# The output loop of an attention and expert kernel: stores moved from ScalarE to SyncE's queue, one load a unit earlier, and the spread of reciprocals ahead of a load

## The chip, the cores and the metric

The kernel runs on 1 core of a Trainium2 chip. The metric is the device time of one execution in microseconds (us), the median of several.

## What is computed

`x` is 8 sequences of 1024 tokens with 256 features. The reference normalises each token and adds to `x` an attention part (16 heads of 64) and a part of 64 experts, 8 to a token, with one shared expert:

```python
x = L0_attn_y
xn = _layernorm(x, axis=-1)
# _L0_attn_ref: per head h, out_h = softmax(q_h k_h^T / 8) v_h; result = concat(out_h) @ Wo.T + bo
# _L0_ffn_ref: routed experts (silu(g) * u @ w_down, weighted, summed over a token's experts) + shared expert
x = x + _L0_attn_ref(xn, ...) + _L0_ffn_ref(xn, ...)
```

## The kernel before, in words

A first stage normalises, routes and computes the values and the shared expert. Then come 64 (`NP`) pairs of heads, 8 to a sequence, in 65 steps written once in `step` for each engine: step s computes the scores, exponentials and value products of pair s, finishes pair s-1 (`fin`) and prepares the following ones. Step 63 is `LAST`, step 64 is `NP`, which has only the finish of pair 63. One expert is computed beside each pair; GpSimd adds its rows to the tensor `moe` in HBM by an indirect DMA. Normalised outputs of a pair go to `ot` in HBM (`store`, L1682, from `out_raw`). To normalise, the sums' reciprocals (`recip`, VectorE, L1385) are spread over the partitions by eight small DMAs (`spread_out`, L1675, into `sum_all`), and VectorE multiplies (L1402).

The output loop multiplies `ot` with Wo. It runs over 16 units (`UNITS`) of 512 tokens; unit u is half `u % 2` of sequence `u // 2`, and its buffers have the parity `par = u % 2`. For each unit:

- SyncE loads the unit's outputs (`load_output`, L1803: two DMAs of 1 MB into `ot32`), and the input x and the expert part of a unit (`load_rest`, L1809 and L1810: 0.5 MB each). In step 63 it loads units 0 and 1, in step 64 units 2 and 3 and the rest of units 0 and 1; in `output()` it loads in each turn unit u and the rest of unit u-2.
- ScalarE rounds the outputs to their high half (`split_high`, L1288, into what were `q_full` and `k_full`; in step 63, for unit 0, `split_piece`, L1280), VectorE subtracts to have the low half (`split_low`, L1483, into `q_rest` and `k_rest`).
- TensorE (`tokens`, L1168) makes for each of 4 groups of 128 tokens 24 matmuls of 128x256, in the order high (`q_full`), low (`q_rest`), high (`k_full`), low (`k_rest`): 96 a unit. Behind unit 0 it makes a constant row (L1180, L1181), which ScalarE copies (L1305).
- GpSimd adds x and expert part (L1641, `rest`), VectorE adds the constant (L1491) and the two banks of PSUM (L1499, into `y`).
- ScalarE issues one DMA of 0.5 MB that stores the unit (`store`, L1296). Each buffer (`ot32`, `x_out`, `moe_sb`, `rest`, `y`) is there twice.

The order is set by each engine's own queue and by semaphores. ScalarE's turn for unit u waits for TensorE's unit u-2 (`y_filled`), splits unit u, and then waits for VectorE's last add of unit u-1 (`y_ready`) to store it; the split of unit u+1 is queued behind that. VectorE's turn is `split_low(u)` twice, then `add_rest(u-1)`. SyncE's `load_output` of unit u waits for the load before it and for `ot_low`, the low halves of unit u-2; `load_rest` of unit u-2 is queued behind it and waits for GpSimd's add of two units before. In step 63 SyncE issues, in this order, the shift DMAs (L1662), `load_output(0, 0, 0)`, a wait for its landing, `load_output(0, 1, 1)` and `spread_out(62)`. VectorE's work in that step behind the reciprocals is: a copy out of PSUM, the first norm (L1402), the gate of the expert (L1408, L1412), the second norm, three sums of exponentials (L1477), the low half of Wo (L1456), another copy (L1394), a low half of unit 0 (L1483), four more sums, and the other low half. TensorE's sums over partitions (L1018) and its last product with the values (L1003) follow these, then unit 0.

Of the kernel before, what the change touches and what calls it, by code (L numbers as in the profile page):

```python
# [26 lines left out]
B, N, D = 8, 1024, 256  # L27
# [4 lines left out]
NP = B * PAIRS  # L32
# [10 lines left out]
UNIT = 4  # L43
UNITS = TILES // UNIT

HIGH, LOW = 0, 1
DMA = 16
# [5 lines left out]
def alone(engine, met, *waits):  # L53
    waits = [(sem, v if isinstance(v, int) else engine.to_reg(v)) for sem, v in waits]
    engine.wait_ge(*met)
    for sem, value in waits:
        engine.wait_ge(sem, value)


def known(v, least):  # L60

    return isinstance(v, int) and v < least
# [651 lines left out]
def is_step(s, n):  # L714

    return isinstance(s, int) and s == n
# [4 lines left out]
LAST = NP - 1  # L721
# [59 lines left out]
def attention_stage(nc, ctx, io, keep):  # L781
# [76 lines left out]
    out_v = io["out"].rearrange("(u t p) d -> u p t d", p=P, t=UNIT)  # L858
# [347 lines left out]
    def _(act):  # L1206
# [81 lines left out]
                nc.scalar.copy(ot(par, HIGH, batch), ot32[par][:, batch * BATCH:(batch + 1) * BATCH]  # L1288
                               ).then_inc(ot_high, 1)

        def store(v, par):

            if not known(v, 1):
                act.wait_ge(y_stored, DMA * v)
            act.wait_ge(y_ready, 2 * (v + 1))
            act.dma_start(out_v[bass.ds(v, 1)].rearrange(parts), y[:, par]).then_inc(y_stored, DMA)  # L1296

        def output():
            def unit(u, par):
                act.wait_ge(y_filled, 2 * (u - 1))  # L1300
                split_high(u, par)
                store(u - 1, 1 - par)

            act.wait_ge(const_filled, 1)
            nc.scalar.copy(const[:], const_ps).then_inc(const_ready, 1)  # L1305
            store(0, 0)
            unit(2, 0)
            unit(3, 1)
            with act.Fori(2, UNITS // 2) as i:
                unit(i * 2, 0)  # L1310
                unit(i * 2 + 1, 1)
            store(UNITS - 1, 1)
            act.wait_ge(y_stored, DMA * UNITS)

        def empty(p):

# [27 lines left out]
    def _(dve):  # L1344
# [141 lines left out]
        def add_rest(u, par):  # L1486

            dve.wait_ge(rest_ready, u + 1)
            if known(u, 1):
                dve.wait_ge(const_ready, 1)  # L1490
            nc.vector.tensor_tensor(rest[:, par], rest[:, par],  # L1491
                                    const[:].rearrange("p (o d) -> p o d", o=1).to_broadcast([P, UNIT, D]), ALU.add
                                    ).then_inc(rest_full, 1)
            if not known(u, 2):
                dve.wait_ge(y_stored, DMA * (u - 1))
            dve.wait_ge(rest_full, u + 1)
            for n in range(2):
                dve.wait_ge(y_filled, 2 * u + n + 1)
                nc.vector.tensor_tensor(y[:, par, 2 * n:2 * n + 2, :],  # L1499
                                        psum[:, banks[par][n], :].rearrange("p (t d) -> p t d", d=D),  # L1500
                                        rest[:, par, 2 * n:2 * n + 2, :], ALU.add).then_inc(y_ready, 1)
# [152 lines left out]
    def _(sp):  # L1654
# [50 lines left out]
        def load_values(p, pp):  # L1705
            sp.dma_start(v_sb[:, pp], one(io["v"], p, "p t c", "(o p) t c")).then_inc(v_loaded, DMA)
# [14 lines left out]
        def step(s, par, flags):  # L1721
            fin, att, nxt, prj = flags
            loads = prj and not (isinstance(s, int) and s == NP - 3)
            p, pp = s + 1, 1 - par
            if is_step(s, LAST - 1):
                sp.wait_ge(lows_ready, 4 * NP)
                sp.dma_start(wo32[:], io["wo"].rearrange("(h p) d -> p h d", p=P)).then_inc(loaded_w, DMA)
                sp.dma_start(bv[:], io["bv"]).then_inc(loaded_b, DMA)
                sp.dma_start(bo[:], io["bo"]).then_inc(loaded_b, DMA)
            if nxt:  # L1730
                waits = [(lows_ready, 4 * (s + 2))]
                if not known(s, 0):
                    waits.append((placed, DMA * SHUFFLES * (s + 1)))
                if not known(s, 1):
                    waits.append((probs_ready, SCORES * s))
                alone(sp, (standing, 1), *waits)
                place(pp)
            if att:
                shift_out(s, par, 1)
            if is_step(s, LAST):  # L1740
                for half in range(2):
                    sp.wait_ge(out_stored[half], DMA * PAIRS)
                sp.wait_ge(placed, DMA * SHUFFLES * NP)
                sp.wait_ge(quad_filled, QUADS * NP)
                load_output(0, 0, 0)
                for n in range(2):
                    sp.wait_ge(ot_loaded[n], DMA)
                load_output(0, 1, 1)
            if nxt:
                waits = []  # L1750
                if not known(s, 0):
                    waits.append((experts_loaded, 3 * DMA * (s + 1)))
                if not known(s, 1):
                    waits.append((y_weighted, s))
                alone(sp, (standing, 1), *waits)
                load_expert(p, pp)
            if nxt:
                waits = []
                if not known(s, 0):
                    waits.append((v_loaded, DMA * (s + 1)))  # L1760
                if not known(s, 1):
                    waits.append((pv_done, 4 * s))
                alone(sp, (standing, 1), *waits)
                load_values(p, pp)
            if fin:
                spread_out(s - 1)
            if is_step(s, NP):
                sp.wait_ge(pv_done, 4 * NP)
                sp.wait_ge(sums_added, 14 * NP - 7)
                sp.wait_ge(last_sums, 7)  # L1770
                sp.wait_ge(scattered, DMA * NP)
                load_rest(0, 0)
                for n in range(2):
                    sp.wait_ge(ot_loaded[n], 2 * DMA)
                sp.wait_ge(ot_low, 2)
                load_output(1, 0, 0)
                sp.wait_ge(xm_loaded, 2 * DMA)
                load_rest(1, 1)
                for n in range(2):
                    sp.wait_ge(ot_loaded[n], 3 * DMA)  # L1780
                sp.wait_ge(ot_low, 4)
                load_output(1, 1, 1)
            if loads:

                alone(sp, (standing, 1), (w_loaded, 2 * DMA * (s + 3)), (lows_ready, 4 * (s + 2) + 2),
                      (x_loaded[0], DMA * x_loads(s + 2)))
                load_weights_of(sp, io, keep, s + 3, pp)
                load_tokens(sp, io, keep, s + 3, 0)
            if fin:
                store(s - 1, 0)  # L1790
            if nxt:
                shift_out(s + 1, pp, 0)
            if fin:
                store(s - 1, 1)
            if loads:
                alone(sp, (standing, 1), (lows_ready, 4 * (s + 2) + 4), (x_loaded[1], DMA * x_loads(s + 2)))
                load_tokens(sp, io, keep, s + 3, 1)


        def load_output(b, half, par):  # L1800

            for n in range(2):
                sp.dma_start(ot32[par][:, n * BATCH:(n + 1) * BATCH],  # L1803
                             io["ot"][bass.ds(b * PAIRS + n * BATCH, BATCH), :, half * HALF:(half + 1) * HALF]
                             .rearrange("h p c -> p h c")).then_inc(ot_loaded[n], DMA)

        def load_rest(u, par):

            sp.dma_start(x_out[:, par], x_v[bass.ds(u, 1)].rearrange(parts)).then_inc(xm_loaded, DMA)  # L1809
            sp.dma_start(moe_sb[:, par], moe_v[bass.ds(u, 1)].rearrange(parts)).then_inc(xm_loaded, DMA)  # L1810

        def output():
            def batch(b):
                for par in range(2):
                    u = b * 2 + par
                    alone(sp, (loaded_w, DMA), (ot_loaded[0], DMA * u), (ot_loaded[1], DMA * u), (ot_low, 2 * (u - 1)))
                    load_output(b, par, par)
                    alone(sp, (loaded_w, DMA), (xm_loaded, 2 * DMA * (u - 2)), (rest_ready, u - 3))
                    load_rest(u - 2, par)

            with sp.Fori(2, B - 1) as b:
                batch(b)
            for half in range(2):
                sp.wait_ge(out_stored[half], DMA * NP)
            batch(B - 1)
            for par in range(2):
                u = UNITS - 2 + par
                sp.wait_ge(xm_loaded, 2 * DMA * u)
                sp.wait_ge(rest_ready, u - 1)
                load_rest(u, par)  # L1830

        head()
        run_steps(sp, step)
# [83 lines left out]
```

## Time and profile before

| | us |
|---|---|
| median of 3 runs | 3481.81 |
| lowest, highest | 3479.49, 3484.37 |
| the profiled execution | 3479.67 |
| its span, first to last instruction | 3477.9 |
| mean granted TensorE clock (share of full) | 0.992 |
| busy: TensorE, VectorE, ScalarE, GpSimd | 3402.9, 2511.5, 1638.7, 2796.8 |

All times of rows are from the start of the span of that one execution; it lies 1.8 us under the execution's own time, and that execution 2.1 us under the median. PE is TensorE's matmuls, PEld its weight loads, DVE VectorE, ACT ScalarE, POOL GpSimd, SPq and ACTq the queues in which SyncE and ScalarE issue DMAs. In a row of the timeline, the square brackets hold the engine's idle time before the instruction and what ended it. Merged rows (x8 and the like) show the first start and the time to the last end.

### The profile page before, as it was taken

The numbers are of one execution on the slowest core, as the hardware profiler recorded it, in microseconds if no ns is written. First come the engines' busy times: TensorE is split into PE (matmuls) and PEld (weight loads), VectorE is DVE, ScalarE is ACT, GpSimd is POOL, SyncE is SP. The second block draws the span as 40 slices with busy tenths as digits, with TensorE's granted clock in tenths as the row PEclk, the third lists the DMA queues.
The fourth block names the chain that finished last, engine by engine and source line by source line (L and its number), as shares of the span: only waits on it lengthen the run. The fifth ranks groups of instructions, "written<-read, shape, count | busy, mean of one in ns | idle before, by whom it ended". The sixth has DMA issues, their size and how long they took to land.

```text
span 3477.9 us, 61694 instructions
## 1 busy us (share of the span) xinstructions
PE 3402.9 (98%) x16978; PEld 2092.4 (60%) x16978; DVE 2511.5 (72%) x3133; ACT 1638.7 (47%) x3086; POOL 2796.8 (80%) x2378
## 2 busy tenths in 40 slices
PE   8999799999999999999999999999999999999988
PEld 6888555555555555555555555555555555555788
DVE  8999567777777777777777777777777777776555
ACT  4666344444444444444444444444444444444322
POOL 3433399999999999999999999999999999999322
PEclk9999899999999999999999999999999999999999
DMA  7887756777777767777767777777777777774676
GB/s 246 250 245 243 183 136 163 189 186 185 184 191 188 186 185 186 186 186 185 184 183 190 191 191 187 185 186 186 185 188 187 184 185 190 188 186 125 215 265 212
DMA packets 424338, 669.26 MB, mean 192 GB/s; under 512 B 63329, under 2 KB 228962, under 8 KB 424290
## 3 DMA queue, kind: packets, MB, share of 16 engines
q1 hardware_dynamic: 401506, 637.20, 66.9%
q0 software_dynamic: 14336, 23.08, 3.4%
q10 hardware_dynamic: 8448, 8.39, 0.7%
q8 instruction: 24, 0.39, 0.0%
q14 instruction: 24, 0.20, 0.0%
HBM read 306.98 MB, written 126.12 MB: 125 GB/s over the span
## 4 chain that ended last, share of the span: by engine, by line
PE 81%; DMA 3%; DVE 3%; issue 1%; SPq 1%; ACT 0%; POOL 0%; ACTq 0%; DVEq 0%; POOLq 0%
PE psum L1003 26%; PE psum L960 15%; PE psum L963 13%; PE psum L1064 10%; PE psum L988 10%; PE psum L1049 2%; DMA probs<-moe 2%; PE psum L1018 2%; PE psum L1168 1%; DVE k_rest L1483 1%; PE psum L1055 1%; PE psum L1056 1%; DVE merged L1356 0%; POOL probs L1641 0%; PE psum L1041 0%
## 5 line engine op out<-in xcount | busy, mean ns | idle before, releaser
L1265 ACT ACTIVATE probs<-psum 128x512 f32<-128x512 f32 x2048 | 1077.3, 603 | 1199.8 <-PE psum L963 1193.0
L1356 DVE TENSOR_REDUCE merged<-psum 128x1 fp32r<-128x1024 f32 x1024 | 1201.1, 1214 | 591.7 <-PE psum L988 582.4
L1610 POOL TENSOR_TENSOR sums<-sums,probs 128x512 f32<-128x512 f32 x762 | 973.6, 1278 | 60.1 <-ACT probs L1265 2.0
L1611 POOL TENSOR_TENSOR sums<-sums,probs 128x512 f32<-128x512 f32 x762 | 975.6, 1280 | 0.0
L1003 PE MATMUL psum<-probs,v_sb 128*64 128x512 f32 x4096 | 937.5, 600 | 0.0
L960 PE MATMUL psum<-q_full,k_full 128*128 128x512 f32 x2048 | 861.4, 421 | 2.5 <-DVE merged L1356 1.6
L963 PE MATMUL psum<-q_rest,k_rest 65*128 65x512 f32 x2048 | 811.7, 396 | 2.9 <-DMA q_rest<-turned 2.9
L1003 PEld LDWEIGHTS psum<-probs,v_sb 128*64 128x64 f32 x4096 | 271.7, 137 | 564.8 <-issue 497.0
L960 PEld LDWEIGHTS psum<-q_full,k_full 128*128 128x128 f32 x2048 | 388.1, 190 | 178.8 <-issue 76.8
L963 PEld LDWEIGHTS psum<-q_rest,k_rest 65*128 65x128 f32 x2048 | 389.8, 190 | 70.9 <-DMA q_rest<-turned 3.2
L1064 PE MATMUL psum<-x_t,w_qk 128*128 128x512 f32 x1536 | 407.3, 401 | 10.2 <-DVE merged L1356 5.8
L988 PE MATMUL psum<-high 64*128 64x512 f32 x2016 | 369.6, 444 | 3.2 <-DVE merged L1356 3.2
L1064 PEld LDWEIGHTS psum<-x_t,w_qk 128*128 128x128 f32 x1536 | 276.5, 190 | 103.5 <-issue 24.0
L988 PEld LDWEIGHTS psum<-high 64*128 64x128 f32 x2016 | 150.1, 184 | 298.7 <-issue 251.0
L1366 DVE SCALAR_TENSOR_TENSOR low<-psum,bias,high 128x512 fp32r<-128x512 f32 x256 | 185.9, 727 | 174.4 <-ACT high L1213 165.6
L1213 ACT ACTIVATE high<-psum,bias 128x512 fp32r<-128x512 f32 x248 | 170.5, 688 | 168.4 <-PE psum L1064 127.2
L1610 POOL TENSOR_TENSOR sums<-probs 128x512 f32<-128x512 f32 x127 | 163.2, 1285 | 89.5 <-ACT probs L1265 87.8
L1385 DVE RECIPROCAL recip<-recip 128x128 f32<-128x128 f32 x256 | 224.2, 917 | 4.8 <-ACT recip L1320 4.8
L1641 POOL TENSOR_TENSOR probs<-probs 128x1024 f32<-128x1024 f32 x16 | 48.6, 3035 | 166.3 <-DMA probs<-moe 163.6
L1611 POOL TENSOR_TENSOR sums<-probs 128x512 f32<-128x512 f32 x127 | 162.0, 1276 | 0.0
L297 POOL TENSOR_TENSOR xt_low<-xt,xt_high 128x512 fp32r<-128x512 f32 x32 | 40.5, 1288 | 146.7 <-ACT xt L377 146.7
L1402 DVE TENSOR_TENSOR out_raw<-out_raw,sum_all 128x512 f32<-128x512 f32 x128 | 147.1, 1150 | 14.5 <-DMA sum_all<-recip 14.5
(171 smaller groups left out, 3389.7 us busy)
## 6 DMA issues: line engine op xcount, KB each, us to landing
x_t<-xt SPq DMA_DIRECT2D x118, 1024.0 KB, 7.1
k_full<-high SPq DMA_DIRECT2D x256, 256.0 KB
v<-values SPq DMA_DIRECT2D x64, 512.0 KB, 3.3
w_qk<-wqk_parts SPq DMA_DIRECT2D x64, 512.0 KB
v_sb<-v SPq DMA_DIRECT2D x64, 512.0 KB, 5.6
q_full<-high SPq DMA_DIRECT2D x128, 256.0 KB
q_full<-low SPq DMA_DIRECT2D x128, 256.0 KB
k_rest<-low SPq DMA_DIRECT2D x128, 256.0 KB
```

The lines of the kernel that those rows point to most:

```text
L960: nc.tensor.matmul(out, k_full[:, par, h, keys], q_full[:, par, h, cols], start=True, stop=False)
L963: nc.tensor.matmul(out, k_rest[0:DK + 1, par, h, keys], q_rest[0:DK + 1, par, half, h, :], start=False, stop=True).then_inc(scores_ready, 1)
L988: last = nc.tensor.matmul(work[:, 2 * h + part, :], high[rows, 1 - par, 0, q * P:(q + 1) * P], high[rows, 1 - par, 1, part * HALF:(part + ...
L1003: last = nc.tensor.matmul(out_ps[rows, :], v_sb[:, par, kt, rows], probs[:, kt, h, :], start=(kt == 0), stop=(kt == KT - 1))
L1064: last = nc.tensor.matmul(out, w_qk[:, par, which, wp, kd, :], x_t[:, xp, kd, cols], start=(j == 0 and kd == 0), stop=(j == 2 and kd == KD ...
L1213: nc.scalar.activation(high[:, par, which, half * HALF:(half + 1) * HALF], work[:, 0, :], ACT.Identity, bias=bias[:, par, which:which + 1] ...
L1265: nc.scalar.activation(probs[:, kt, h, :], score_bank(j), ACT.Exp, scale=SCALE).then_inc(probs_ready, 1)
L1356: nc.vector.tensor_reduce(out=merged[:, q // GROUP, col:col + 1], in_=work[:, 2 * h:2 * h + 2, :].rearrange("p b c -> p (b c)"), axis=AX, ...
L1366: nc.vector.scalar_tensor_tensor(out=low[:, par, which, cols], in0=bank, scalar=bias[:, par, which:which + 1], in1=f32(high[:, par, which, ...
L1385: nc.vector.reciprocal(recip[:, cols], recip[:, cols]).then_inc(recip_ready, 1)
L1610: nc.gpsimd.tensor_tensor(total[:, 0, :], first[:, 0, :], probs[:, kt, 0, :], ALU.add)
L1611: nc.gpsimd.tensor_tensor(total[:, 1, :], first[:, 1, :], probs[:, kt, 1, :], ALU.add).then_inc(sums_added, 1)
```

## The change

ScalarE's `store` is gone. SyncE stores instead, in two halves of 256 tokens, each waiting for VectorE's add of that half and for the landing of the half stored before; in the turn that loads the outputs of unit u it stores unit u-4, and x and expert part are now those of unit u-1, not u-2. VectorE's `add_rest` of unit u waits for both halves of unit u-2. The last four units are stored behind the loop. In step 63 `spread_out(62)` is issued ahead of the wait for the first outputs and of `load_output(0, 1, 1)`; in step 64 `load_output(1, 0, 0)` is issued ahead of `spread_out(63)`, and `load_rest(2, 0)` is added at the end.

```diff
             def unit(u, par):
                 act.wait_ge(y_filled, 2 * (u - 1))
                 split_high(u, par)
-                store(u - 1, 1 - par)
...
             if not known(u, 2):
-                dve.wait_ge(y_stored, DMA * (u - 1))
+                dve.wait_ge(y_stored, 2 * DMA * (u - 1))
...
                 load_output(0, 0, 0)
-                for n in range(2):
-                    sp.wait_ge(ot_loaded[n], DMA)
-                load_output(0, 1, 1)
...
+            if is_step(s, NP):
+                for n in range(2):
+                    sp.wait_ge(ot_loaded[n], 2 * DMA)
+                sp.wait_ge(ot_low, 2)
+                load_output(1, 0, 0)
             if fin:
                 spread_out(s - 1)
+            if is_step(s, LAST):
+                for n in range(2):
+                    sp.wait_ge(ot_loaded[n], DMA)
+                load_output(0, 1, 1)
             if is_step(s, NP):
...
                 load_rest(0, 0)
-                for n in range(2):
-                    sp.wait_ge(ot_loaded[n], 2 * DMA)
-                sp.wait_ge(ot_low, 2)
-                load_output(1, 0, 0)
                 sp.wait_ge(xm_loaded, 2 * DMA)
                 load_rest(1, 1)
...
                 load_output(1, 1, 1)
+                sp.wait_ge(xm_loaded, 2 * 2 * DMA)
+                sp.wait_ge(rest_ready, 1)
+                load_rest(2, 0)
...
+        def store_output(v, par, half):
+
+            waits = [(y_ready, 2 * v + half + 1)]
+            if not known(2 * v + half, 1):
+                waits.append((y_stored, DMA * (2 * v + half)))
+            alone(sp, (loaded_w, DMA), *waits)
+            tokens = slice(half * UNIT // 2, (half + 1) * UNIT // 2)
+            sp.dma_start(out_v[bass.ds(v, 1), :, tokens, :].rearrange(parts), y[:, par, tokens]).then_inc(y_stored, DMA)
+
         def output():
...
+            def unit(b, u, par):
+                alone(sp, (loaded_w, DMA), (ot_loaded[0], DMA * u), (ot_loaded[1], DMA * u), (ot_low, 2 * (u - 1)))
+                load_output(b, par, par)
+                alone(sp, (loaded_w, DMA), (xm_loaded, 2 * DMA * (u - 1)), (rest_ready, u - 2))
+                load_rest(u - 1, 1 - par)
+                for half in range(2):
+                    store_output(u - 4, par, half)
...
+            for v in range(UNITS - 4, UNITS):
+                for half in range(2):
+                    store_output(v, v % 2, half)
+            sp.wait_ge(y_stored, 2 * DMA * UNITS)
```

## Rows read from the trace of the kernel before

**Rows 1.** The page, part 4: chain that ended last, by engine.

```profile
PE 81%; DMA 3%; DVE 3%; issue 1%; SPq 1%; ACT 0%; POOL 0%; ACTq 0%; DVEq 0%; POOLq 0%
```

**Rows 2.** Busy us by windows (PE, PEld, DVE, ACT, POOL), granted clock, DMA share, GB/s.

```profile
3258.00:3285.00 27.00, 27.00 (x210) 25.72 (x208) 14.27 (x11) 4.09 (x3) 4.79 (x2) 1.00 0.87 285
...
3368.00:3395.00 27.00, 24.77 (x192) 24.36 (x192) 15.50 (x11) 7.44 (x4) 6.31 (x2) 0.94 0.78 272
```

**Rows 3.** Timeline of the output loop: start us, us, engine, line, operation, count.

```profile
3274.00 0.37 ACT L1305 COPY const<-psum 128x256 f32<-128x256 f32 x1 [17.13 <-PE psum L1181]
...
3284.73 1.87 SPq L1803 DMA_DIRECT2D ot<-ot  x2
...
3285.36 1.11 PE L1168 MATMUL psum<-x_t,q_full 128*128 128x256 f32 x8
...
3296.72 1.11 PE L1168 MATMUL psum<-x_t,q_full 128*128 128x256 f32 x8
...
3369.36 0.95 SPq L1803 DMA_DIRECT2D ot<-ot  x2
...
3370.45 1.29 DVE L1499 TENSOR_TENSOR probs<-psum,probs 128x512 f32<-128x512 f32 x2 [0.21 <-DVE probs L1491]
...
3376.54 2.29 DVE L1483 TENSOR_TENSOR k_rest<-ot,k_full 128x2048 fp32r<-128x2048 f32 x1
...
3473.11 0.63 PE L1168 MATMUL psum<-x_t,k_rest 128*128 128x256 f32 x4
```

**Rows 4.** Timeline of step 63 and behind; third row from the chain.

```profile
3214.32 3.39 DVE L1385 RECIPROCAL recip<-recip 128x128 f32<-128x128 f32 x4 [4.78 <-ACT recip L1320]
...
3222.88 5.17 SPq L1675 DMA_DIRECT2D sum_all<-recip  x8
...
3227.46 5.25 DMA sum_all<-recip
...
3231.25 1.13 ACT L1265 ACTIVATE probs<-psum 128x512 f32<-128x512 f32 x2
...
3235.51 1.05 POOL L1594 TENSOR_TENSOR silu_e<-up_gate,silu_e 128x256 f32<-128x256 f32 x1 [2.78 <-DVE silu_e L1412]
...
3245.36 5.20 DVE L1477 TENSOR_TENSOR sums<-sums,probs 128x1024 f32<-128x1024 f32 x4
...
3250.70 1.93 PE L1018 MATMUL psum<-sums,ones 128*32 128x512 f32 x8 [3.53 <-DVE sums L1477]
...
3252.56 5.77 PE L1003 MATMUL psum<-probs,v_sb 128*64 128x512 f32 x16
```

**Rows 5.** Groups by line, 3258 to 3478: busy us, mean ns, idle before.

```profile
L1168 PE MATMUL psum<-x_t,k_rest 128*128 128x256 f32 x256 | 43.1, 292 | 15.9 <-DVE k_rest L1483 15.9
```

**Rows 6.** Windows of one microsecond, columns as in rows 2.

```profile
3370.00:3371.00 1.00, 1.00 (x7) 1.00 (x7) 0.79 (x2) 0.00 (x0) 0.00 (x0) 0.50 0.35 53
...
3385.00:3386.00 1.00, 1.00 (x11) 1.00 (x10) 0.91 (x2) 0.00 (x0) 0.00 (x0) 1.00 1.06 399
```

**Rows 7.** Chain of waits in time, one double unit: start us, us, what.

```profile
3371.29 10.64 DMA probs<-moe
...
3382.09 2.40 POOL probs L1641
...
3387.28 0.38 ACTq L1296
...
3388.09 1.92 ACT q_full L1288
...
3392.24 4.48 DVE k_rest L1483
...
3398.90 10.57 DMA probs<-moe
```

**Rows 8.** DMA issues, KB each, median us to landing: 3190-3260, then 3260-3478.

```profile
ot<-out_raw SPq DMA_DIRECT2D x4, 256.0 KB, 2.0
...
out_y<-probs ACTq DMA_DIRECT2D x16, 512.0 KB, 4.7
```

More of the change, by code:

```diff
@@ L1289, in split_high @@
                                ).then_inc(ot_high, 1)
[L1291 to L1296, printed above, removed]
         def output():
@@ L1301, in unit @@
                 split_high(u, par)
-                store(u - 1, 1 - par)
             act.wait_ge(const_filled, 1)
             nc.scalar.copy(const[:], const_ps).then_inc(const_ready, 1)
[L1306 to L1309, printed above, removed]
+            with act.Fori(1, UNITS // 2) as i:
                 unit(i * 2, 0)
                 unit(i * 2 + 1, 1)
-            store(UNITS - 1, 1)
-            act.wait_ge(y_stored, DMA * UNITS)
         def empty(p):
@@ L1810, in load_rest @@
             sp.dma_start(moe_sb[:, par], moe_v[bass.ds(u, 1)].rearrange(parts)).then_inc(xm_loaded, DMA)
-        def output():
[L1813 to L1822, printed above, removed]
+        def store_output(v, par, half):
[5 more added lines that the diff above has]
+            sp.dma_start(out_v[bass.ds(v, 1), :, tokens, :].rearrange(parts), y[:, par, tokens]).then_inc(y_stored, DMA)
@@ new lines, in output @@
+        def output():
+            def unit(b, u, par):
[5 more added lines that the diff above has]
+                    store_output(u - 4, par, half)
+            unit(2, 4, 0)
+            unit(2, 5, 1)
+            with sp.Fori(3, B - 1) as b:
+                unit(b, b * 2, 0)
+                unit(b, b * 2 + 1, 1)
@@ L1823, in output @@
             for half in range(2):
                 sp.wait_ge(out_stored[half], DMA * NP)
[L1825 to L1830, printed above, removed]
+            unit(B - 1, UNITS - 2, 0)
+            unit(B - 1, UNITS - 1, 1)
+            sp.wait_ge(xm_loaded, 2 * DMA * (UNITS - 1))
+            sp.wait_ge(rest_ready, UNITS - 2)
@@ L1832, in _ @@
+            load_rest(UNITS - 1, 1)
+            for v in range(UNITS - 4, UNITS):
+                for half in range(2):
+                    store_output(v, v % 2, half)
+            sp.wait_ge(y_stored, 2 * DMA * UNITS)
         head()
```

## The prediction, made before the changed kernel was run

> **What bounds the kernel now.** I read the page's shares of the chain first: 81% of the span is TensorE, so an edit pays only where TensorE waits [rows 1]. The change touches the step before the last and the loop behind it, from about 3205 us to the end at 3477.9. In that loop the table of windows has DMA engines 0.87 busy at 285 GB/s while TensorE is never idle, and 0.78 later, where it is [rows 2]. A unit of 96 matmuls without a wait takes 3296.72 - 3285.36 = 11.36 us [rows 3]. Sixteen of them and the constant row (3274.0 - 3258.3 - 11.36 less 0.2 for the copy's start: some 4.1 us) would take 185.9 us, but the loop runs from 3258.3 (the last product with the values ends there, 3252.56 + 5.77) to 3473.7: 215.4 us [rows 3, 4]. The 29.5 us of excess are the subject. The groups by line name what TensorE waits for: the low half of the last operand, k_rest, 15.9 us in the matmul rows [rows 5]. The rest is mostly matmuls at 1.2 GHz behind these waits; after the one at 3369 the granted clock of a microsecond is 0.50 [rows 6].
>
> The chain of waits says why k_rest is late. It repeats every 27.6 us, which is two units: expert part on its way 10.64 us, GpSimd's add 2.40, VectorE's adds, the store issued by ScalarE at 3387.28, and only behind it ScalarE's split at 3388.09, then VectorE's low halves (4.48 us for the second, beside a GpSimd add, against 2.29 alone) [rows 3, 7]. Ahead of the next load of x and expert part on SyncE's queue stands the load of the next unit's outputs, which waits for those low halves. So it is a ring: load, add, store, split, low half, load. 13.8 us a unit against 11.36.
>
> **Part 1, the last full step.** Step 63 issues eight small spreads of reciprocals. They stand ready at 3214.32 + 3.39 = 3217.7, but SyncE waits for a 2 MB load, issues another 2 MB and only then the spreads, at 3222.88; the last lands at 3227.46 + 5.25 = 3232.7 [rows 4]. After the change they are issued from 3217.75 to 3222.9 with nothing of size ahead but the first load, and land some 2.0 us behind the last issue, the landing of a 256 KB transfer with a free queue [rows 8]: 3224.9 at the latest. That is 8 us, but not all of it reaches the end. Behind it VectorE has two norms and the reciprocals of the gate (about 3.3 us), then three sums that need exponentials, the last of them done at 3231.25 + 1.13 = 3232.4 [rows 4]. So: third sum done 3233.9, low part of the output weights 2.28, a copy out of PSUM 0.68, a low half 2.28, four sums 5.20: 3244.3, against 3245.36 + 5.20 = 3250.6. That is 6.2 us earlier. On TensorE the expert's second product waits for a GpSimd product at 3235.51, which could start 2.78 us earlier, when GpSimd's sums end; with it the scores come as much earlier, and the product behind them ends by 3243, in time. Bounds: contention with GpSimd for two VectorE operations takes 1.1 back (5.1 gained); if TensorE's clock stays high over the shorter gap, the 1.93 and 5.77 us of sums and last product, which ran at the low level, give back 3 more (9.2) [rows 4]. I take 6.0, near the sums' own rows. The second output load goes out 1 us later than before; it is used 20 us later, so this costs nothing.
>
> **Part 2, the head of the loop.** ScalarE no longer waits for the first store, so the split of unit 2 follows the constant, 3274.00 + 0.37 less 6.0 = 3268.4. VectorE ends its adds at about 3271.0 and the two low halves at 3275.6, or 3277.8 with GpSimd's third add beside the second of them. The load of unit 4 waits for them: I take 3277.0 against 3284.73 [rows 3].
>
> **Part 3, the steady loop.** Removed: ScalarE's 16 stores and their waits, which stood ahead of 13 splits. ScalarE needs 3.8 us a unit, VectorE some 7 (two low halves of 2.3, 1.3 for the adds out of PSUM, as much for the constant's) and GpSimd 2.4 [rows 3, 7], so none of them is a new bound. Added on SyncE's queue: a unit is now the load of outputs (2.1 MB), x and expert part of the unit before (1.05 MB), and the two halves of a store of four units back (0.52 MB), each half waiting until the half before it has landed. The bytes do not change: 3.67 MB a unit.
>
> What changes is who stands behind whom. SyncE waits at the second half for the landing of the first, and the next unit's load of outputs stands behind that wait. In the trace, the eight spreads of step 63, 64 KB each, with a 2 MB load issued just ahead, took 5.25 us for the last one to land, against 2.0 for a larger transfer alone [rows 4, 8]: a small transfer issued behind a large one on SyncE's queue comes out behind it. So the first half lands when the 3.1 MB of the same unit have. The nearest row for the time of such a burst from a standing start: load issued at 3369.36, expert part issued last and landed at 3371.29 + 10.64 = 3381.93, that is 12.6 us for the same 3.67 MB, the store on ScalarE's queue among them [rows 3, 7]. At 3370 the engines moved 53 GB/s, at 3385 399 [rows 6]: the start-up is in it, and in the changed loop the queue runs nearly dry in each unit, so it is paid each time. With 0.3 us for wake-up and registers the unit takes **12.9 us**, set by SyncE, not by TensorE's 11.36.
>
> The Trainium skill ("DMA: Bandwidth & Descriptors", section "Queues, rings and completion order") says that SyncE and ScalarE each own one row of rings on the same 16 engines, that an engine goes round the rows, and that within a ring descriptors are consumed in order. It speaks against moving the stores: on ScalarE's row a store got its turn beside the loads, on SyncE's it stands behind them. By it the first half lands at the burst's end (the 12.9 us here); were the engines free to take it early, the unit would be TensorE's 11.36 us.
>
> VectorE's adds for a unit wait for both halves of the store of two units back. The second lands 2.0 us behind its issue, at 12.4 + 2.0 = 14.4 us after the unit's load of outputs; the adds (1.3) and both low halves (4.6) follow, so k_rest of the unit is ready 20.3 us after its load. It is a delay, not a ring: the load that depends on it is two units on, and 20.3 over two units is 10.2, under 12.9.
>
> **Sum.** Load of unit 15: 3277.0 + 11 x 12.9 = 3418.9; its k_rest 3439.2; the rest of unit 15 without waits 9.0: 3448.2; from the last matmul to the end of the span 3477.9 - 3473.74 = 4.2, as now [rows 3]: 3452.4. That is 25.5 us below the span of 3477.9, so 3454.2 for the profiled execution's 3479.67, and 3456.3 against the median of 3481.81, which is 2.1 above the profiled one. **Forecast 3456 us.**
>
> **Rivals.**
> (a) *TensorE is the bound.* A half of a store lands early, or the burst is faster than the row because loads are issued closer together. It decides below 12.05 us a unit. Then 3252.3 + 185.9 + 4.2 = 3442.4, 35.5 below: 3446. For it: at the 399 GB/s of 3385 the 3.67 MB take 9.2 us; against it: the start-up at 3370 [rows 6].
> (b) *The loop keeps its old pace.* Start-up, writes in the same ring and skew between engines make it 13.8 us a unit; only the head and part 1 pay, and the delay grows by 0.9: 3452.4 + 9.9 + 0.9 = 3463.2, 14.7 below: 3467.
> (c) *Slower.* A half of a store at the ring's end does not overlap with the reads ahead: it starts when they have landed and takes a store's own 4.7 us, the median landing on ScalarE's queue [rows 8]. Then 12.6 + 4.7 + 0.3 = 17.6 us a unit, 11 x 4.7 = 52 more than the forecast: 3508. It makes the kernel slower from 15.2 us a unit on. Against it: 4.7 is mostly queueing beside loads, and 256 KB alone land in 2.0.
> (d) *Part 1 does nothing*, because another wait (the exponentials, the low half of unit 0) sets the sums: 6 us less gain, 3462; it moves a forecast inside the range rather than making a case of its own.
>
> **Chances.** Forecast, with a pace of 12.2 to 13.4 and (d) within it: 0.52. (a) 0.25, (b) 0.15, (c) 0.06, and 0.02 for no change from some wait I overlooked. The measurement can tell some 0.2% (7 us) from no change. Faster by more: 0.91; within: 0.03; slower: 0.06. The range takes in (a) and (b) and leaves out (c): 3443 to 3468. The forecast's own: 3449 to 3463.
>
> **What would show it.** Part 1: the first norm of step 63 at about 3225, the last sum's end near 3244 and the first output matmul near 3252. Part 3: issues of the output load 12.9 us apart, each right behind the landing of the first half of a store; ScalarE's splits waiting for TensorE or the load and no more for VectorE's adds; VectorE's adds released by the landed store. TensorE waits for k_rest each unit, 1.5 us, instead of each second. If those issues come every 11.4 us with TensorE unbroken, (a) holds; if the first half lands over 15 us behind its unit's load, the forecast has the wrong sign.

## The result: 3460 us, and what the profile after shows

| | us |
|---|---|
| the changed kernel, median of 4 runs | 3460.18 |
| the kernel before on the same chip, median of 4 | 3483.09 |
| ratio, with 95% interval | 0.9934 (0.9920 to 0.9947) |
| span of the changed kernel's profiled execution | 3462.3 |
| forecast, range | 3456, 3443 to 3468 |

22.9 us less by the medians, where 25.5 were forecast. All medians and ratios here and below leave out two executions that fell far outside the rest, one of `act_halves` (5136 us) and one of the kernel before beside it (15641 us). A comparison of two spans mixes in the 63 steps ahead, which nothing in the change touches and which differ by some us between executions. I therefore count from a mark: the start of the shift DMAs in step 63, 3209.63 before and 3214.28 after. From there to the end of the span it was 268.3 us and is 248.0: 20.3 less. By the same count the forecast had 242.8, 25.5 less.

The steady loop first, on SyncE's queue in the changed kernel (start us, us from first start to last end, engine, line, operation, count). L1795 is the output load, L1801 and L1802 the loads of x and expert part, L1811 the halves of the store:

```profile
3349.93 1.00 SPq L1795 DMA_DIRECT2D ot<-ot  x2
3351.25 0.37 SPq L1801 DMA_DIRECT2D probs<-in_x  x1
3351.72 0.60 SPq L1802 DMA_DIRECT2D probs<-moe  x1
3352.68 9.83 SPq L1811 DMA_DIRECT2D out_y<-probs  x2
3363.20 0.99 SPq L1795 DMA_DIRECT2D ot<-ot  x2
```

The first half is issued at 3352.68, the second at 3362.1 (3352.68 + 9.83 less its own 0.40), and 0.7 us behind the end of that issue comes the next unit's load. From the load at 3297.30 to that at 3427.11 it is ten units of 12.98 us; the forecast had 12.9. What SyncE waits for in the window 3297 to 3428 (waiter, releaser: us in total, times, longest), first before, then after:

```profile
SPq L57 <- DVE k_rest L1483: 48.0, 8, 9.3
```

```profile
SPq L57 <- DMA out_y<-probs: 71.1, 10, 7.5
```

The wait for VectorE's low half, which closed the ring of [rows 7], is gone, and the landing of a half of a store stands in its place. The DMA engines stand still behind it in each unit (windows of one microsecond; the last three columns are granted clock, DMA share, GB/s):

```profile
3362.00:3363.00 1.00, 1.00 (x11) 1.00 (x10) 0.00 (x0) 0.00 (x0) 1.00 (x1) 1.00 0.00 0
...
3366.00:3367.00 1.00, 1.00 (x11) 1.00 (x10) 1.00 (x1) 0.00 (x0) 0.00 (x0) 1.00 1.06 406
```

The engines behind it, timeline of the changed kernel:

```profile
3377.20 1.29 DVE L1486 TENSOR_TENSOR probs<-psum,probs 128x512 f32<-128x512 f32 x2 [5.98 <-DMA out_y<-probs]
...
3380.75 0.74 PE L1168 MATMUL psum<-x_t,q_rest 128*128 128x256 f32 x4 [0.40 <-DVE q_rest L1470]
...
3380.79 1.92 ACT L1288 CAST q_full<-ot 128x2048 fp32r<-128x2048 f32 x1 [7.80 <-DMA ot<-ot]
...
3382.95 0.74 PE L1168 MATMUL psum<-x_t,k_rest 128*128 128x256 f32 x4 [0.52 <-DVE k_rest L1470]
```

VectorE's adds are released by the landed store, after 5.98 us of waiting; ScalarE's split waits for the load and no more for VectorE; from 3355 on TensorE stops twice in nearly every unit, for well under a microsecond each time, where the forecast had one stop of 1.5 us. The short stops paid a second time, through the clock. The same stretch of both kernels, before and then after (busy us of PE, PEld, DVE, ACT, POOL with counts; clock, DMA share, GB/s):

```profile
3297.00:3428.00 131.00, 115.13 (x902) 113.09 (x902) 76.04 (x48) 33.93 (x19) 31.66 (x10) 0.95 0.74 258
```

```profile
3297.00:3428.00 131.00, 125.23 (x1034) 122.78 (x1033) 68.24 (x50) 41.37 (x22) 24.74 (x11) 1.00 0.84 282
```

TensorE stood for 15.9 us of 131 and ran part of the rest at 1.2 GHz; now it stands for 5.8 and the granted clock is 1.00. The groups by line say the same (busy us, mean ns, idle before), against [rows 5]:

```profile
L1168 PE MATMUL psum<-x_t,k_rest 128*128 128x256 f32 x256 | 41.7, 285 | 4.1 <-DVE k_rest L1470 4.1
L1168 PE MATMUL psum<-x_t,q_rest 128*128 128x256 f32 x256 | 41.5, 284 | 4.2 <-DVE q_rest L1470 4.1
```

**Step 63**, the counterpart of [rows 4], in the changed kernel:

```profile
3222.47 5.00 SPq L1662 DMA_DIRECT2D sum_all<-recip  x8
...
3229.82 1.56 DVE L1389 TENSOR_TENSOR out_raw<-out_raw,sum_all 128x512 f32<-128x512 f32 x1 [6.86 <-DMA sum_all<-recip]
...
3235.68 2.30 DVE L1464 TENSOR_TENSOR sums<-probs 128x1024 f32<-128x1024 f32 x1
...
3238.08 3.79 DVE L1464 TENSOR_TENSOR sums<-sums,probs 128x1024 f32<-128x1024 f32 x2
...
3244.79 1.19 PE L1055 MATMUL psum<-w_d,hidden_e 128*128 128x256 f32 x2 [3.78 <-POOL hidden_e L1584]
...
3247.06 5.20 DVE L1464 TENSOR_TENSOR sums<-sums,probs 128x1024 f32<-128x1024 f32 x4
...
3249.32 4.16 PE L1003 MATMUL psum<-probs,v_sb 128*64 128x512 f32 x16
...
3253.42 1.07 PE L1018 MATMUL psum<-sums,ones 128*32 128x512 f32 x8
...
3254.41 3.65 PE L1003 MATMUL psum<-probs,v_sb 128*64 128x512 f32 x16
```

The first three sums in the kernel before, 26.3 us from the mark instead of 21.4, but shorter:

```profile
3235.89 1.75 DVE L1477 TENSOR_TENSOR sums<-probs 128x1024 f32<-128x1024 f32 x1
...
3237.74 2.68 DVE L1477 TENSOR_TENSOR sums<-sums,probs 128x1024 f32<-128x1024 f32 x2
```

From the mark, the first norm starts at 15.5 us (23.1 before, 7.6 earlier), the last sum ends at 38.0 (40.9, 2.9 earlier), the first output matmul starts at 43.7 (48.6, 4.9 earlier).

### The profile page after: what moved, and what is told of

It is laid out like the page before. It is cut to its first block and busy times, and to the rows that moved or that the text cites. A ratio compares the mean times of both kernels' runs of the same rounds, so it can differ in the third digit from the quotient of the medians.

```text
span 3462.3 us, 61727 instructions
## 1 busy us (share of the span) xinstructions
PE 3399.4 (98%) x16978; PEld 2088.4 (60%) x16978; DVE 2505.0 (72%) x3133; ACT 1640.8 (47%) x3086; POOL 2794.0 (81%) x2378
## 5 line engine op out<-in xcount | busy, mean ns | idle before, releaser
L1003 PE MATMUL psum<-probs,v_sb 128*64 128x512 f32 x4096 | 935.9, 599 | 0.0
L1003 PEld LDWEIGHTS psum<-probs,v_sb 128*64 128x64 f32 x4096 | 271.4, 136 | 562.9 <-issue 483.5
L1353 DVE SCALAR_TENSOR_TENSOR low<-psum,bias,high 128x512 fp32r<-128x512 f32 x256 | 185.9, 727 | 175.1 <-ACT high L1213 166.6
L1628 POOL TENSOR_TENSOR probs<-probs 128x1024 f32<-128x1024 f32 x16 | 40.0, 2500 | 160.2 <-DMA probs<-moe 160.2
```

The costliest lines, as they stand in the source:

```text
L1003: last = nc.tensor.matmul(out_ps[rows, :], v_sb[:, par, kt, rows], probs[:, kt, h, :], start=(kt == 0), stop=(kt == KT - 1))
L1353: nc.vector.scalar_tensor_tensor(out=low[:, par, which, cols], in0=bank, scalar=bias[:, par, which:which + 1], in1=f32(high[:, par, which, ...
```

## The experiments

Each was read in two ways: by its time against the kernel before on the same chip, and by its trace, from the mark to the first and to the last output matmul, with the mean distance of the output loads from unit 5 to unit 15 (the last column). The second is free of the 63 steps ahead, but it is one execution. Each ratio is to the kernel before on the same chip; its medians there were 3482.21 to 3483.94, and the row "before" has the one of the start.

| kernel | median us | ratio to before (95%) | first output matmul | last ends | us a unit |
|---|---|---|---|---|---|
| before | 3481.81 | | 48.6 | 264.1 | 13.9 |
| changed | 3460.18 | 0.9934 (0.9920-0.9947) | 43.7 | 242.7 | 13.0 |
| changed_again | 3462.99 | 0.9946 (0.9932-0.9959) | 42.7 | 241.0 | 13.0 |
| one_store | 3450.09 | 0.9906 (0.9891-0.9921) | 43.5 | 229.8 | 11.4 |
| halves_free | 3449.60 | 0.9903 (0.9887-0.9920) | 42.5 | 228.8 | 11.2 |
| quarters | 3510.28 | 1.0081 (1.0059-1.0102) | 42.7 | 281.5 | 16.1 |
| act_halves | 3444.39 | 0.9891 (0.9869-0.9912) | 44.0 | 230.3 | 11.3 |
| act_later | 3450.40 | 0.9910 (0.9892-0.9928) | 46.2 | 232.5 | 11.1 |
| one_store_rest_late | 3446.29 | 0.9898 (0.9880-0.9916) | 44.1 | 230.4 | 11.3 |
| old_spread | 3468.04 | 0.9956 (0.9942-0.9969) | 48.5 | 243.3 | 12.8 |
| only_spread | 3479.63 | 0.9995 (0.9985-1.0005) | 43.3 | 259.6 | 13.9 |
| one_store_old_spread | 3453.15 | 0.9909 (0.9893-0.9926) | 47.8 | 234.1 | 11.4 |
| act_later_spread | 3450.63 | 0.9900 (0.9883-0.9916) | 43.9 | 230.2 | 11.2 |

**Control.** 

> The changed kernel itself, as a measure for the others on this chip: 22 to 23 us below the kernel before, as in its first runs.

Measured 3462.99, the ratio 0.9946: some 19 us below the kernel before, three less than expected, though the two intervals overlap. The last output matmul ends at 241.0 against 242.7. Medians of one kernel on two chips differ by some 3 us, and nothing smaller is read out of them below.

**Is it SyncE's wait or the DMA engines' time?** One DMA stores a unit:

```diff
-                for half in range(2):
-                    store_output(u - 4, par, half)
+                store_output(u - 4, par)
```

> The changed kernel with each unit stored by one DMA of 0.5 MB on SyncE's queue instead of two halves, so that no store of a unit waits for the landing of another store of the same unit; bytes, order and queue stay. Theory (SyncE's wait for the first half, with the next output load behind it, sets 13.0 us a unit): the loads are issued without that wait, the pace falls to TensorE's 11.36, TensorE runs without a break from its first output matmul (3258.0 + 185.9 = 3443.9 instead of 3457.1): 13 us less than the changed kernel, some 3447. Rival (the DMA engines need 13 us for 3.67 MB with the start-ups, whoever waits): same as the changed kernel within 2 us, 3460. Rival 2 (SyncE is released but ring order delays VectorE's adds, so that k_rest is the wait): between, 3452 to 3458.

3450.09, 13 us below the control as expected, and TensorE runs through: 229.8 - 43.5 = 186.3 us from first to last output matmul, where sixteen units of 11.36 and the constant make 185.9. The rivals fall. SyncE's queue in that kernel:

```profile
3343.61 0.95 SPq L1795 DMA_DIRECT2D ot<-ot  x2
3344.91 0.37 SPq L1801 DMA_DIRECT2D probs<-in_x  x1
3345.38 0.65 SPq L1802 DMA_DIRECT2D probs<-moe  x1
3346.39 1.41 SPq L1810 DMA_DIRECT2D out_y<-probs  x1
3354.95 0.93 SPq L1795 DMA_DIRECT2D ot<-ot  x2
```

But this edit took away a wait and also made the transfers larger. So the next one keeps the halves and takes only the wait, by giving each half its own semaphore:

```diff
-            if not known(2 * v + half, 1):
-                waits.append((y_stored, DMA * (2 * v + half)))
+            if not known(v, 1):
+                waits.append((y_stored[half], DMA * v))
```

> The changed kernel with two semaphores for the stores, one for first and one for second halves, so that a half waits only for the same half of the unit before, long landed. Sizes, halves, queue and order are those of the changed kernel; the landing wait inside the unit is all that goes. Theory: 11.4 us a unit and the last matmul 11 to 13 us earlier than in the changed kernel, as with one store. Rival (it was the halving of the store, more and smaller transfers in the ring, and not the wait): 12.5 to 13 us a unit.

3449.60 and 11.2 us a unit: the wait is the whole of it, and the size of the transfers makes no difference that can be seen while TensorE is the bound. (The edit gives VectorE's wait for the stores the two semaphores as well.) Its stretch 3297 to 3428 has TensorE busy throughout, with the same bytes at 316 GB/s:

```profile
3297.00:3428.00 131.00, 131.00 (x1110) 131.00 (x1109) 83.09 (x57) 42.57 (x23) 34.32 (x12) 1.00 0.94 316
```

**The wait tripled.** Four quarters, each behind the landing of the one before:

```diff
-                for half in range(2):
-                    store_output(u - 4, par, half)
+                for t in range(UNIT):
+                    store_output(u - 4, par, t)
```

> The changed kernel with each unit stored in four quarters of 0.13 MB, each waiting for the landing of the one before: the suspected wait tripled, the bytes the same. Theory (landings in SyncE's queue set the pace): the first quarter lands with the burst, the next two some 2.3 us after their issue plus 0.4 each, so 13.0 + 5.4 = 18.4 us a unit, and the kernel some 55 to 60 us slower than the changed one, 3515 to 3520: slower than before. Rival (DMA throughput sets the pace, the waits are beside it): 13 to 14 us a unit.

3510.28 (two executions), slower than before, so this chain can turn the sign; 16.1 us a unit, not 18.4. The direction is the theory's, the price was not: the two more landings make the unit 3.1 us longer, where I had 5.4. In the unit that is loaded at 3363.61, the second quarter goes out 11.5 us behind the load (12.2 for the second half above), the third and fourth 1.9 and 1.8 us behind the one before. So a landing with its issue cost 1.9, not 2.7, and the first wait became 0.7 shorter. In the window 3300 to 3400 a quarter lands a median 1.7 us behind its issue (line, KB each, us to landing), where I had 2.3:

```profile
out_y<-probs SPq DMA_DIRECT2D x25, 128.0 KB, 1.7
```

**The same wait on another queue.** Halves, each waiting for the half before, issued by ScalarE behind its split:

```diff
                 split_high(u, par)
+                for half in range(2):
+                    store_half(u - 2, par, half)
```

> The changed kernel with the same halves and the same wait of one half for the landing of the other, but issued by ScalarE on its own queue, behind the split of a unit and for the unit two behind. Theory (what costs is that the next output load stands behind the wait on SyncE): SyncE's loads are free of it, the pace is TensorE's 11.4 us unless ScalarE's split of the next unit comes late behind its second half; ScalarE has 7.5 us to spare in a unit and a half lands in some 5 beside loads, so 11.4 to 12 and 3447 to 3455. Rival (halves are bad for the DMA engines on whichever queue): 13 us a unit as in the changed kernel.

The stores are gone from SyncE's queue, and on ScalarE's they come two units behind, not four. 3444.39, 11.3 us a unit, TensorE busy for all 131.00 us from 3297 to 3428, though a half still lands a median 6.0 us behind its issue (window 3300 to 3400; 8.7 in the changed kernel). So a landing wait did no harm by itself here. It did where the load that feeds the next unit was queued behind it.

**Was the move needed at all?** The kernel before, with the store one unit further behind and nothing else:

```diff
                 split_high(u, par)
-                store(u - 1, 1 - par)
+                store(u - 2, par)
```

> The kernel before with one edit: ScalarE stores unit u-2 instead of unit u-1 behind the split of unit u; stores stay whole and on ScalarE's queue, loads of x and expert part stay two units behind, step 63 is as before. Theory (the ring load, add, store, split, low half, load is closed by the store's place on ScalarE): the ring opens, k_rest is ready some 20 us behind its load over two units, so the pace is TensorE's 11.4 us and the kernel 25 to 30 us faster than before: 3452 to 3457. Rival (the late load of x and expert part closes the ring by itself, through VectorE's adds ahead of the low halves): 13 to 13.8 us a unit, 0 to 10 us faster than before.

3450.40: this edit in the kernel before takes more than the whole change. By the ratios it is 31 us, a little over the 25 to 30 expected, against 19 to 23, and its interval overlaps that of one of the two sets of runs of the changed kernel; by the traces the last output matmul ends at 232.5 against 242.7 and 241.0. Its groups say who waits for what in the stretch 3290 to 3440 (waiter, releaser: us, times, longest):

```profile
ACT q_full L1288 <- PE psum L1168: 68.9, 9, 7.7
DVE probs L1491 <- POOL probs L1641: 52.9, 12, 9.9
```

ScalarE's split waits for TensorE, whose operand buffer it overwrites; VectorE still waits for GpSimd, which waits for the late load of x and expert part (111.0 us in 14 waits), and TensorE is busy for 131.00 of the 131 us between 3297 and 3428. The ring was closed by the store's place on ScalarE. The late load takes part in it only through that store.

> The kernel with one store a unit on SyncE's queue, and x and expert part loaded two units behind as before the change. Theory (the earlier load is not needed once the store no longer holds ScalarE): k_rest some 20 us behind its load over two units is 10, under 11.36, so the pace stays 11.4 and the kernel within 3 us of the one with the earlier load, 3447 to 3453. Rival (the earlier load opens the ring): 12.5 us a unit or more, at least 12 us slower than with it.

That kernel is one_store with `load_rest(u - 2, par)` in the turn of unit u and `load_rest(2, 0)` left out of step 64. 3446.29 and 11.3 us a unit: the earlier load of x and expert part brings nothing that can be measured once the store no longer holds ScalarE.

**Step 63 alone, and undone.** `load_output(0, 1, 1)` ahead of `spread_out` as before, in the changed kernel (old_spread), and behind it, in the kernel before (only_spread):

```diff
                 load_output(0, 0, 0)
+                for n in range(2):
+                    sp.wait_ge(ot_loaded[n], DMA)
+                load_output(0, 1, 1)
```

> The changed kernel with the order of step 63 as before: wait for the first outputs and second output load ahead of the spread of reciprocals. Theory (part 1 is worth what the traces show between the start of the step and the first output matmul, 48.7 against 43.8 us): 4.9 us slower than the changed kernel. Rival (the start of the loop is set by the constant and the loads, or the pace swallows it): within 1 us of the changed kernel.

> The kernel before with the new order of step 63 alone. Theory: the loop begins 4.9 us earlier and keeps its 13.8 us a unit, so 4.9 us faster than before. Rival (the gain of part 1 comes only with the new loop): within 1 us of before.

The times settle neither: 5.1 us between old_spread and the control by the medians, with overlapping intervals; 0.9995 (0.9985 to 1.0005) for only_spread, which is 2 us and leaves room for 5 or for none. The traces say more. Alone in the kernel before, the new order brings the first output matmul 5.3 us and the last 4.5 us earlier. In the changed kernel it brings the first 4.8 to 5.8 earlier, the last only 0.6 to 2.3. One reading was that SyncE's pace takes the gain back, so the next pair has TensorE as its bound:

> One store a unit, with the order of step 63 as before. In the changed kernel the traces gave part 1 only 1 to 2.4 us at the last matmul, though 5 at the first. Theory (there SyncE's pace, not TensorE, decides, and takes the gain back): where TensorE is the bound the first output matmul 48.5 us and the last 234.8 us behind the reference mark, that is 5 us later than with the new order (43.5 and 229.8), at both ends. Rival (part 1's gain is lost whatever the loop): 230 to 231 at the last matmul.

4.3 us later at both ends, where 5 were expected (47.8 and 234.1 against 43.5 and 229.8): there the gain passes through whole. For the changed kernel it stays open how much is lost and how much is chance: in old_spread unit 4 is loaded 3.8 to 4.3 us later than in the two executions with the new order, and most of that is made up by a mean pace of 12.8 against 13.0 in these executions.

**Two small edits together.** act_later and only_spread in one kernel:

> The kernel before with two small edits: ScalarE stores unit u-2 instead of unit u-1 behind its split, and step 63 in the new order. Theory (both edits add up where TensorE bounds the loop): first output matmul at 43 to 44, last at 229 to 231 us behind the reference mark, 3446 to 3448, as good as one store on SyncE's queue. Rival (without the move to SyncE something of the gain is missing): 3451 or more.

From the mark it does what was expected: 43.9 and 230.2. The median does not: 3450.63 lies above the expected 3446 to 3448 and just short of the rival's 3451, with a ratio of 0.9900 (0.9883 to 0.9916), which does not tell it from act_later (0.9910); its profiled execution reached the mark only at 3217.8, 3 to 9 us behind the others. Six kernels, one_store, halves_free, act_halves, act_later, one_store_rest_late and this one, lie some 10 to 16 us below the changed kernel. By their intervals none of them is better than another.

## Why the prediction was right, step by step

Counted from the mark, the forecast had the end at 242.8 and it came at 248.0. By its own terms:

- **Pace of SyncE, 12.9 us a unit.** Measured 12.98 over ten units, and halves_free shows that it is this wait. That the number comes so close is in part luck, for two errors cancel inside. The burst was shorter than the 12.6 us of [rows 7]: the second half goes out 12.2 us behind the load in the unit shown (3349.93 to 3362.1) and 12.1 in the mean of the ten, landing and wake-up included. The row that I took it from moved 3.67 MB, but only 3.4 MB have to land here, since the second half is not yet issued. The way from there to the next load was longer than the 0.3 us I gave it: 1.1 us in the unit shown (a DMA issue of 0.40 and 0.7 for registers and waits), 0.9 in the mean. The first turn, 14.8 us, I had at 12.9: the loads of x and expert part of unit 2, the last ones of step 64, were still on their way, and GpSimd could start on them only at 3284.90 (DMA share 1.05 from 3275 to 3288). This term was 2.7 us short over eleven turns.
- **Load of unit 4.** 68.2 us from the mark, 67.4 in the forecast. The 1.1 us that part 1 fell short, below, are in this.
- **k_rest 20.3 us behind its load.** For unit 15: 3445.42 + 2.28 - 3427.11 = 20.6. The rest of the unit 9.3 instead of 9.0.
- **The tail.** I took the 4.2 us of before. It is 5.3, from the last matmul at 3457.0 to 3462.3, since the last eight halves wait for one another there too; in halves_free, where they don't, it is 3.4. SyncE's and VectorE's last rows:

```profile
3441.96 18.14 SPq L1811 DMA_DIRECT2D out_y<-probs  x8
...
3457.05 0.69 DVE L1486 TENSOR_TENSOR probs<-psum,probs 128x512 f32<-128x512 f32 x1 [2.71 <-PE psum L1168]
```

The last half was issued at 3459.7, two us behind the add that it waits for. These five, 0.8 + 2.7 + 0.3 + 0.3 + 1.1, are the 5.2 us.

**Part 1 was 6.0, measured 4.9, and its inside was wrong.** The spreads landed when I said. But of 7.6 us the sums kept 2.9, not 6.2: the step from the landed spreads to the sums is where this part failed. I allowed 1.1 us for two VectorE operations beside GpSimd; moved forward, nearly all of them up to the low half of Wo fall beside its sums and its gate. The norm of 0.69 us took 1.56, the first sum 2.30 against 1.75, the next two 3.79 against 2.68, against 1.30 a sum alone. GpSimd was slowed in turn (its last product for the expert took 2.49 us, 1.42 before), so the expert's second product came 30.5 us from the mark, not 2.8 us earlier than before but 0.6 later (29.9 there). The product with the values behind it, which I had "in time" at 3243, or 33.4 from the mark, ended at 39.2 (3249.32 + 4.16), 1.2 us behind the last sum. TensorE reached the sums over partitions only behind it, at 3253.42, and that took 1.0 us of the gain away. (In changed_again the product and the last sum end 0.2 us apart.) The other 3.0 us are TensorE's clock: the sums over partitions and the last product with the values (L1018, L1003) took 1.07 and 3.65 us instead of 1.93 and 5.77. Before, TensorE had stood for 3.53 us just ahead of them [rows 4] and they ran at 1.2 GHz; in the changed kernel it had not stopped since the 3.78 us ahead of 3244.79, and the granted clock, 0.50 from 3247 to 3250, was 1.00 from 3251 on. So 4.9 is 2.9 - 1.0 + 3.0, and that it lies near 6.0 is luck. Nor is the clock's share surely the edit's. act_later has the old order of step 63, stood for 1.72 us there and ran these at full clock as well, with its first output matmul at 46.2; the four executions with the old order, the kernel before among them, lie at 46.2 to 48.6, the nine with the new at 42.5 to 44.1. Nor did the sum's assumption hold that part 1 reaches the end whole: the traces of the changed kernel have 0.6 to 2.3 us of it at the last output matmul, and why is open.

**The rivals.** (a) needed under 12.0 us a unit (the 12.05 of the prediction is a slip: 10.0 us over 11 turns is 0.91 below 12.9); what kept it off is the one wait that halves_free removes, and with it gone the kernels lie near the 3446 of (a). (b) was the old pace: no. (c) wanted a landing 17.3 us behind the load; it came by 12.2, so its mechanism did not occur. A slower kernel by landings was still near: quarters, with three waits a unit, has 16.1 us, past my turning point of 15.2, and ends its last output matmul at 281.5 against 264.1 before. (d), that part 1 does nothing, is wrong for the first output matmul (4.9 us) and nearly right for the last.

**Ring order.** The rule of the Trainium skill on rings ("DMA: Bandwidth & Descriptors", section "Queues, rings and completion order") was weighed right for the changed kernel, and the trace agrees: the first half lands with the burst ahead of it, by 12.2 us behind the load. But the late landing cost nothing by itself: halves_free puts the same halves in the same queue, where they land a median 8.5 us behind their issue (8.7 in the changed kernel, window 3300 to 3400), at 11.2 us a unit.

## What to carry to other kernels

When a store moves to the queue that issues the loads, look at what it waits for, and what stands behind that wait: here a wait for a landing cost the whole burst queued ahead of it, in each turn, and a semaphore for each half, so that neither waits for the other, removed it here. Before moving work to another queue, ask which single wait closes the ring; here, storing one unit later on the same queue opened it. And work that is moved forward off a stall falls beside what ran there already: cost it by the rows of both engines busy, not by those of one alone.

## What the runs showed that I had not expected

- TensorE's granted clock stayed at 1.00 while it stopped eleven times between 3354 and 3422, for 0.4 to 0.6 us each. Before, the four stops of 2.7 us from 3297 to 3428 each went with a clock of 0.50 behind them, that of 2.42 us at 3313 did not, and the mean was 0.95.
- The DMA engines moved 326 GB/s over 131 us in act_later, with loads on one queue and stores on the other, 316 in halves_free with all on one, and 282 in the changed kernel: at shares of 0.94, 0.94 and 0.84. They were the bound in none: in the first two TensorE was busy for all 131 us, and in the third the DMA engines stood still in each unit.
- The price of a landing went with what was ahead in the ring. In quarters, where three stores of four have nothing ahead, 128 KB took a median 1.7 us. In the changed kernel the first half of a unit, behind 3.1 MB, is landed some 9 us after its issue (3352.68 to 3362.1, wake-up included).
